# Two attentions: the transfers of the maxima's rows are issued by ScalarE in place of SyncE

## What is computed

```python
def _L0_xattn_ref(x, y, bias, Wq, Wk, Wv, Wo):      # 16 heads of depth 8
    q = _split_heads(x @ Wq); k = _split_heads(y @ Wk); v = _split_heads(y @ Wv)
    logits = jnp.einsum('bhqd,bhkd->bhqk', q * scale, k) + bias
    weights = jax.nn.softmax(logits, axis=-1)
    ...
    return attn @ Wo
```

## Time and profile before

| | us |
|---|---|
| three timed runs | 1490.34, 1495.89, 1503.8 |
| their median | 1495.89 |
| the profiled execution | 1489.75 |
| its span | 1488.0 |

### The profile page before, as it was taken

The page is one execution under the profiler, slowest core; times in us unless marked ns, Lnnn a source line. Parts: engine busy times, 40 slices in busy tenths (PEclk is TensorE's granted clock), DMA queues, the critical chain, the costliest instruction groups (busy, mean ns, idle before and its releaser), DMA issues. The chain is left out here.

```text
span 1488.0 us, 21408 instructions
## 1 busy us (share of the span) xinstructions
PE 965.2 (65%) x6394; PEld 564.5 (38%) x6396; DVE 661.4 (44%) x2199; ACT 487.1 (33%) x975; POOL 443.7 (30%) x690
## 2 busy tenths in 40 slices
PE   4699998779685899367777129992297100799400
PEld 2233333435463565223333116661165000677300
DVE  6588885433334333655663303333355700233222
ACT  2478877412211232244554003330233000233100
POOL 2424320046103004155552340005300177000375
PEclk8599999779857999567885559996598555799755
DMA  5345544000130111233431011111110011355212
GB/s 191 100 140 187 173 144 141 7 0 0 44 130 25 36 42 40 79 100 114 145 117 58 22 46 41 41 41 45 53 36 2 7 51 53 107 143 146 80 53 67
DMA packets 110219, 113.39 MB, mean 76 GB/s; under 512 B 11738, under 2 KB 92396, under 8 KB 108980
## 3 DMA queue, kind: packets, MB, share of 16 engines
q1 hardware_dynamic: 100900, 96.04, 20.8%
q0 software_dynamic: 7168, 14.69, 3.3%
q10 hardware_dynamic: 2064, 1.57, 0.3%
HBM read 66.78 MB, written 45.09 MB: 75 GB/s over the span
## 5 line engine op out<-in xcount | busy, mean ns | idle before, releaser
L1726 POOL DMA_INDIRECT e_back<-rows_out,e_pos x112 | 105.9, 945 | 390.0 <-DMA rows_out<-e_y 356.8
L1717 POOL DMA_INDIRECT rows_in<-xn,e_pos x112 | 109.4, 977 | 257.2 <-DVE e_pos L1879 143.8
L651 DVE TENSOR_REDUCE a_neg_max<-bank 128x1 f32<-128x512 f32 x256 | 163.0, 684 | 44.6 <-PE bank L846 42.6
L711 ACT ACTIVATE wb<-bank 128x512 f32<-128x512 f32 x256 | 145.3, 599 | 48.9 <-PE bank L868 48.4
L1969 PE MATMUL bank<-ident,e_xs 128*128 128x128 f32 x192 | 55.8, 294 | 154.6 <-DMA e_xs<-rows_in 150.4
L2075 DVE COPY e_xT<-bank 128x128 f32<-128x128 f32 (+1 forms) x96 | 40.3, 419 | 174.8 <-PE bank L1969 173.1
L646 DVE CUSTOM_DVE_ANT_0 bank<-bank,a_tri 128x128 f32<-128x128 f32 (+1 forms) x256 | 84.4, 388 | 54.8 <-PE bank L841 54.0
L868 PE MATMUL bank<-a_QS,a_KS 51*128 51x256 bf16 x512 | 94.1, 281 | 15.5 <-DMA a_QS<-a_m_rows 8.4
L846 PE MATMUL bank<-a_KS,a_QS 48*128 48x512 bf16 x256 | 98.7, 419 | 7.0 <-DMA a_QS<-a_q_dram 6.2
L1969 PEld LDWEIGHTS bank<-ident,e_xs 128*128 128x128 f32 x192 | 28.3, 148 | 163.4 <-issue 160.9
L886 PE MATMUL bank<-wb,a_V 128*9 128x256 f32 x1024 | 80.6, 389 | 7.4 <-ACT wb L711 5.8
(11 more groups left out here) (284 smaller groups left out, 2062.2 us busy)
## 6 DMA issues: line engine op xcount, KB each, us to landing
rows_in<-wa SPq DMA_DIRECT2D x8, 1024.0 KB, 9.3
wa<-in_f_w SPq DMA_DIRECT2D x8, 1024.0 KB, 7.3
e_xs<-rows_in SPq DMA_DIRECT2D x32, 256.0 KB, 2.9
rows_out<-e_y SPq DMA_DIRECT2D x32, 256.0 KB, 2.3
a_KS<-a_k_dram SPq DMA_DIRECT2D x32, 192.0 KB
wa<-in_f_w SPq DMA_DIRECT2D x8, 768.0 KB, 7.0
wb<-in_f_w SPq DMA_DIRECT2D x8, 768.0 KB, 10.3
a_QS<-a_q_dram SPq DMA_DIRECT2D x56, 96.0 KB
```

The costliest lines, as they stand in the source:

```text
L651: nc.vector.tensor_reduce(least, a_bank[(2 * n + t) % 3][:, :], AX.X, ALU.max, negate=True).then_inc(max_done, 1)
L711: nc.scalar.activation(E[:, h % EBUFS, 512 * u:512 * u + 512], b_bank[u][:, :], ACT.Exp).then_inc(exp_done, 1)
L1717: pool.indirect_dma_start(out=c.rows_in[:, :], out_offset=bass.IndirectOffsetOnAxis(ap=pos[:, K * t + j:K * t + j + 1], axis=0), in_=c.xn[ ...
L1726: pool.indirect_dma_start(out=back[:, n % BACK, :], out_offset=None, in_=rows_out[:, :], in_offset=bass.IndirectOffsetOnAxis(ap=pos[:, n:n ...
```

## The change

`aug_in` leaves SyncE's program and goes to ScalarE's: each call stands right behind the `keep_max` of the same half batch, before the loop and at heads 4 and 12. It waits for the copy's own semaphore, as SyncE did, and in addition for the logits that last read these rows of `QS` (on SyncE this was implied by what stood ahead). SyncE's two conditions for stack_in(i + 2, .) fall together. Sizes, patterns and semaphores of the transfers stay.

```diff
@@ SyncE
-                def aug_in(b, g):
-                    p = b % 2
-                    reach(sp, rows_m, 2 * b + g + 1)
-                    for par in range(2):
-                        sp.dma_start(QS[64 * par + QROWS:64 * par + AUG, p, 4 * g:4 * g + 4, :],
-                                     m_rows[12 * par:12 * par + 12, g, :]).then_inc(aug[p][g], 16)
-
...
                 load_ctx(2)
-                aug_in(0, 0)
                 for i in range(B):
-                    aug_in(i, 1)
...
                         stack_in(i + 2, 0)
-                    if i + 1 < B:
-                        aug_in(i + 1, 0)
-                    if i + 2 < B:
                         stack_in(i + 2, 1)
@@ ScalarE
+                def aug_in(b, g):
+                    p = b % 2
+                    reach(act, rows_m, 2 * b + g + 1)
+                    reach(act, logits_b, NB * (H * (b - 2) + 8 * g + 8))
+                    for par in range(2):
+                        nc.scalar.dma_start(QS[64 * par + QROWS:64 * par + AUG, p, 4 * g:4 * g + 4, :],
+                                            m_rows[12 * par:12 * par + 12, g, :]).then_inc(aug[p][g], 16)
...
                 keep_max(0, 0)
+                aug_in(0, 0)
                 exps(0, 0)
...
                         if h == LAG + 1:
                             keep_max(i, 1)
+                            aug_in(i, 1)
...
                         if h == LAG + 9 and i + 1 < B:
                             keep_max(i + 1, 0)
+                            aug_in(i + 1, 0)
```

## The result

| | before | changed |
|---|---|---|
| median of the timed runs, us | 1495.89 (3 runs) | 1543.33 (3 runs: 1542.51 to 1543.44) |
| profiled execution's span, us | 1488.0 | 1541.6 |
| mean granted clock of TensorE | 0.785 | 0.75 |

The ratio is 1.031 with a 95% interval of 1.0235 to 1.0385. The change costs 47 us where I forecast 16, and the result lies outside the range of 1490 to 1524. The direction of the sum was right, its size was not.

What follows compares the result with a forecast made beforehand. TensorE and ScalarE hold each other in layer 0; rows' transfers are late in layer 2 and at layer 0's start. Terms -3.7 + 12.4 + 7.4 + 7.1 - 7.6 + 2.5 - 1.8 = +16.3 us; predicted 1508, range 1490 to 1524.

Steps and rivals of the forecast that it cites:

- The price of an issue: ScalarE's queue: a pair of issues takes 1.57 us, so an exponential behind a rows' copy begins 1.77 us later.
- Layer 0, the stall: Layer 0's loop: late exponentials delay TensorE, 12.4 us lost at head 12 and 7.4 us at head 4.
- Layer 0, the start: Layer 0's first rows leave earlier, until the context's transfer (ctxT of batch 2) gates project_k(2): 3.7 us gained.
- TensorE's clock: Layer 0: lulls of 2.04 us halve the clock six times at 1.19 us each, 7.1 us lost, bounds 0 and 9.5.
- What SyncE does without its waits: SyncE's queue: losing 64 issues and the waits between them brings nothing, as its next steps wait for later events.
- Layer 2's gain of 6.9 us: Layer 2: earlier rows gain 7.6 us at head 12 and 1.8 at the start, less 2.5 lost at head 4.
- that the clock holds: Rival 0.27: layer 0's lulls leave TensorE's clock full, so the 7.1 us drops out: +9.2 us, 1499 us.
- that the stall is hidden: Rival 0.10: issues on ScalarE cost little or TensorE catches up in layer 0: -13 us, 1477 to 1483 us.
- The third: Rival 0.13: nothing won at both layers' starts, every lull costs a clock fall: +24 to +29 us, 1514 to 1525.

Runs made afterwards that it cites:

- m_l2_free: Kernel before, but ScalarE issues the rows' transfers in layer 2 only, and SyncE doesn't wait for the copies there; 1.0003 of the kernel before.
- a4_fill: Changed kernel plus two float32 matmuls nobody reads, behind head 13 in layer 0, filling TensorE's lull; 1.0203 of the kernel before, median 1527.32 us.
- a6_paced_fill: Changed kernel with SyncE's waits for the rows' copies kept and two unread matmuls filling layer 0's lull behind head 13; 1.0203 of the kernel before, median 1527.35 us.
- m_l0_only: Kernel before, but ScalarE issues the rows' transfers in layer 0 only; SyncE issues in layer 2 and keeps its waits; 1.0307 of the kernel before, median 1541.66 us.
- a1_paced: Changed kernel, but SyncE still waits for the rows' copies where it issued their transfers before; 1.0272 of the kernel before, median 1536.69 us.
- m_l2_waits: Kernel before, but ScalarE issues the rows' transfers in layer 2 only, and SyncE keeps its waits for the copies; 1.0022 of the kernel before.
- m_bestfill: Kernel before; ScalarE issues only each layer's first half batch and layer 2's head 12; unread matmuls fill layer 2's waits for rows; 0.9918, median 1486.86 us.
- m_start: Kernel before, but ScalarE issues only the very first half batch's rows of each layer; 0.9969 of the kernel before.
- m_half: Kernel before, but in layer 0 ScalarE issues one of each half batch's two transfers and SyncE the other; 1.0128 of the kernel before, median 1515.17 us.

## Why the prediction was wrong, point by point

The main error needs two windows: the first batch's stretch from head 4 to head 12 in layer 0, in the kernel before and, with the same program in that layer, in m_l2_free (the granted clock is the third number from the end):

```profile
64.55:79.08 14.53, 13.60 (x135) 5.17 (x132) 10.72 (x20) 10.21 (x22) 5.77 (x17) 0.86 0.41 126
```

```profile
63.66:76.29 12.63, 11.70 (x134) 4.24 (x132) 10.67 (x20) 10.05 (x22) 6.83 (x18) 1.00 0.46 141
```

- **The price of an issue**: right. A pair 1.49 us (1.57), the exponential 1.71 us later (1.77), from ScalarE's own rows. The section of the Trainium skill that the prediction set against it ("DMA: Bandwidth & Descriptors", Anatomy of one DMA) describes the path of transfers that GpSimd issues, so its 50 ns were carried over to ScalarE's queue without a ground; there two issues took 1.43 and 1.49 us.
- **Layer 0, the stall**: right. 7 x 1.73 = 12.1 us at head 12 (12.4); at head 4 0.6 in the first batch (a distance that varies from 12.6 to 15.3 us with the clock, so this is not measured), five times 1.0, 0.4 for batch 6 (14.33 for 13.97 where the rows are in time) and 1.7 for the last, 7.7 in all (7.4). Sum 19.8 us, as forecast. a4_fill and a6_paced_fill, where the clock holds at head 12, bear it out: 14.95 us for 13.22.
- **Layer 0, the start**: right in its mechanism, the context as the next gate included; 2.6 us for 3.7. The gate opened at 53.5 and not at 52.5.
- **TensorE's clock: the step that failed.** I put down six falls of 1.19 us, 7.1 us with 9.5 as a bound. Of the 24.8 us at head 12, 12.7 are not stall; a4_fill, which filled the lull, had none of them. In layer 0's last part the half clock took 8 us more. That is about 20 us. The number of falls was not far off (five in seven lulls, and the last part; six and seven of seven in m_l0_only and a1_paced), the price of one was: three short ones at 1.5 us, two long ones at 4.1, and 8 for the last. I had taken 1.19 us from the one stretch at half clock of the kernel before. That was mis-sized: I set the first batch's 14.53 us beside a later batch's 13.34, and the two don't hold the same work. At full clock the first batch's stretch takes 12.63 us (the windows above). The fall cost 1.90 us for 4.1 us at half clock, 0.46 for each. The new falls are near that rate, 1.5 us for 3.3 at half clock and 4.1 for 10.3, and below it in the last part, 8 for 24. Above all a fall lasted 10 and 24 us, which nothing in that one row could tell. My bounds multiplied this row, so that the range had no room for a dearer fall.
- **What SyncE does without its waits**: a claim that failed in its place. I wrote that it brings nothing; in batches 6 and 7 it released the weights' shares, and rows landed 6.8 us late. At the place it cost 3 to 8 us in layer 2 (15 to 16 us for 8 to 12). For layer 0 (15.7 and 16.95 us for 14.33) it is not shown, since kernels with all of SyncE's waits there took 16.45 and 18.78. That the total suffered from it is not shown: a1_paced's interval overlaps the changed kernel's, and m_l2_free is no slower than m_l2_waits.
- **Layer 2's gain of 6.9 us**: failed. The waits for the rows were halved as forecast, and the start came as forecast (first distance 13.15 to 11.69 us, 1.5 for 1.8), yet m_l2_waits is at 1.0022. The layer's length varies with the clock, 155 to 162 us for one and the same program, and no saved time is left of the saved waits. The prediction had no term for that. What made the clock low in one execution and high in the next was not settled; that filling the lulls raises it m_bestfill shows.
- **The rivals**: that the clock holds fell with the windows and with a4_fill, that the stall is hidden with the lull of 2.00 us. The third, with every lull a fall and no start, gave at most 1525; its direction was right, and it too used the price of 1.19.
- The total adds up. By timed runs: m_l0_only 1.0307 and m_l2_free 1.0003 against 1.031 for both. By the two profiled executions, 53.6 us apart: start -2.8, stall 19.8, clock at head 12 and in the last part 20.7, batch 6 2.6, layer 2 9.2, the stretches outside 3.9, together 53.4. The 47 us of the medians are less, since the profiled execution of the kernel before was a fast one.

## What to carry to other kernels

An issue of a transfer is 0.75 us of the issuing engine's time and sits in its order: put it on an engine that is not the pace, or only at the places where the other queue is late (m_start wins about 0.3%, the whole change loses 3.1%). When a change opens a lull in a tight loop on TensorE, price the lull twice, once as time and once as the clock that may fall behind it, and take the price of a fall from the same stretch of the loop with and without it; a stretch that only looks alike gave 1.19 us here where the fall cost 1.90. A wait that is removed from a queue may also have paced what stands behind it; read that queue to its last iteration.

## What was not expected of the hardware

TensorE's granted clock fell behind five of seven lulls of 2.0 us in a loop that is otherwise some 90% busy (4.7 of 5 us in many windows), and in m_half behind one of seven of 1.26 us; it then stayed at 1.2 GHz for 3 to 10 us. Behind an eighth lull it stayed there for 24 us, with TensorE busy 22.2 of them. Two products that nobody reads, 1.13 us of work in each of the seven lulls of 2.0 us, kept it at 2.4 GHz from the third copy of the rows to the last (1.00 in every window) and made the kernel about 1% faster than the same kernel without them (1.0203 and 1.031 of before). In a6_paced_fill, with the same products, it fell once, behind a wait of 1.87 us for rows. In layer 2 three such products a batch gave a mean clock of 0.86, where the kernels without them had 0.60 to 0.77.
